# First operands of an attention loaded during the stage before it, ones written elsewhere, duplicate stores of q dropped

## The reference, cut to what matters

```python
scores = jnp.einsum('bhqd,bhkd->bhqk', qh, kh) * scale          # A
scores = scores * decay[None, None, :, :]
attn = jax.nn.softmax(scores, axis=-1)
...
scores = jnp.einsum('bhqd,bhkd->bhqk', q, k) / jnp.sqrt(jnp.float32(HD))   # B, after rope
scores = jnp.where(causal, scores, -jnp.inf)
attn = jax.nn.softmax(scores, axis=-1)
```

## Time and profile before

| | us |
|---|---|
| three runs of the kernel | 3136.64, 3138.38, 3142.13 |
| their median | 3138.38 |
| span of the profiled execution, first to last instruction | 3131.4 |

### The profile page before, as it was taken

One profiled execution on the slowest core, in us unless ns is written; L12 is line 12 of the kernel. 1 busy time (PEld: TensorE's weight loads), 2 busy tenths in 40 slices (PEclk: granted clock), 3 DMA queues, 4 the chain that ended last, 5 costly groups with the idle time before them and its releaser, 6 DMA issues. The chain is left out here.

```text
span 3131.4 us, 129400 instructions
## 1 busy us (share of the span) xinstructions
PE 2658.5 (85%) x53553; PEld 1508.1 (48%) x53553; DVE 2510.0 (80%) x7597; ACT 1876.0 (60%) x3797; POOL 1754.7 (56%) x1984
## 2 busy tenths in 40 slices
PE   5884999999999999973340899999999999999998
PEld 2441333333333333363230566666666666666665
DVE  4676899999998999766706788888888888888886
ACT  5783899999999999821000455455555555555553
POOL 5871222222222222341063788888888888888886
PEclk9895999999999999986565999999999999999999
DMA  4676344333333343094023000000000000000000
GB/s 135 235 261 178 73 106 94 93 93 99 93 90 96 94 106 94 27 276 122 0 43 89 10 12 11 8 8 11 11 11 11 11 11 11 11 11 5 11 8 11
DMA packets 179263, 209.94 MB, mean 67 GB/s; under 512 B 28592, under 2 KB 140144, under 8 KB 178416
## 3 DMA queue, kind: packets, MB, share of 16 engines
q1 hardware_dynamic: 176112, 200.25, 23.1%
q0 software_dynamic: 2560, 1.35, 0.4%
HBM read 125.10 MB, written 75.63 MB: 64 GB/s over the span
## 5 line engine op out<-in xcount | busy, mean ns | idle before, releaser
L829 ACT ACTIVATE at_pA<-at_ps 128x512 f32<-128x512 f32 x1024 | 551.9, 614 | 83.8 <-DVE at_ps L882 77.1
L891 DVE CUSTOM_DVE_ANT_0 at_junk<-at_ps,w_cmask 128x512 f32<-128x512 f32 (+3 forms) x1024 | 463.4, 485 | 104.4 <-PE at_ps L732 97.1
L882 DVE TENSOR_TENSOR at_ps<-at_ps,w_ratio 128x128 f32<-128x128 f32 (+3 forms) x1024 | 451.2, 491 | 4.7 <-PE at_ps L726 3.1
L701 POOL TENSOR_SCALAR_AFFINE_SELECT at_pB<-at_pB 128x128 f32<-128x128 f32 x256 | 75.4, 294 | 639.6 <-ACT at_pB L835 637.5
L835 ACT ACTIVATE at_pB<-at_ps 128x512 f32<-128x512 f32 (+1 forms) x768 | 379.4, 531 | 53.0 <-PE at_ps L739 47.7
L1980 POOL TENSOR_TENSOR sc_rb<-sc_rb,v_sin 128x512 f32<-128x512 f32 x256 | 326.6, 1276 | 37.6 <-DVE sc_ra L2220 36.2
L2016 PE MATMUL sc_ps<-sc_xT,v_wqkv 128*128 128x512 f32 x512 | 286.1, 641 | 3.9 <-PEq L56 1.4
L726 PE MATMUL at_ps<-at_aq,at_ak 72*128 72x512 bf16 x1024 | 278.3, 388 | 2.7 <-DMA at_ak<-parts_scratch 2.4
L2179 ACT COPY sc_skN<-sc_ps 128x512 f32<-128x512 f32 x128 | 75.1, 587 | 323.6 <-PE sc_ps L2068 323.6
L1975 POOL TENSOR_TENSOR sc_sk<-sc_ee,sc_relu 128x512 f32<-128x512 f32 x128 | 167.0, 1304 | 180.5 <-ACT sc_ee L2170 180.3
L739 PE MATMUL at_ps<-at_bq,at_bk 75*128 75x512 bf16 (+3 forms) x1024 | 265.7, 302 | 1.5 <-ACT at_pB L835 0.9
(11 more groups left out here) (316 smaller groups left out, 5937.4 us busy)
## 6 DMA issues: line engine op xcount, KB each, us to landing
parts_scratch<-fr_parts SPq DMA_DIRECT2D x64, 384.0 KB, 4.1
at_bq<-parts_scratch SPq DMA_DIRECT2D x192, 96.0 KB
at_bk<-parts_scratch SPq DMA_DIRECT2D x192, 96.0 KB
at_aq<-parts_scratch SPq DMA_DIRECT2D x192, 96.0 KB
at_ak<-parts_scratch SPq DMA_DIRECT2D x192, 96.0 KB
v_scratch<-fr_v SPq DMA_DIRECT2D x32, 352.0 KB, 4.3
at_v<-v_scratch SPq DMA_DIRECT2D x32, 352.0 KB, 3.6
parts_scratch<-fr_parts SPq DMA_DIRECT2D x32, 256.0 KB, 3.9
```

Of the source, the lines that this page charges most:

```text
L829: act.activation(pA[:, n % A_RING, j * S:(j + 1) * S], src, ACT.Exp).then_inc(exped, 1)
L882: dve.tensor_tensor(src[:, 0:wide], src[:, 0:wide], W["ratio"][:, S - wide:S], ALU.mult).then_inc(tilted, 1)
L891: ins = dve.tensor_tensor_reduce(junk[:, P * j * (j + 1) // 2:P * (j + 1) * (j + 2) // 2], src[:, col:col + wide], W["cmask"][:, S - wide: ...
```

## The change

A new function `first_operands` takes buffers for A's group 0 and for B's groups 0 and 1, and the semaphores of all groups' loads, ahead of `front`, and both stages get them as `O`. All groups now have buffers of their own in place of a slice of one tensor. In `front`, DVE writes the ones of B's groups 0 and 1 first of all, and SP at the end of step 3 issues the loads of these three pairs, 24 transfers, all of batch 0. In `attend`, POOL writes the ones of B's groups 2 to 5, one tile after another, and SP's first loads are A group 1, v of batch 0, B group 2, v of batch 1, B groups 3 to 5, each of B's behind its tile's ones. `parts_scratch` has three slots in place of five, the second store of q is gone, and the rotated copies 1 and 2 of q are loaded by two transfers each (16 and 8 rows, or 8 and 16), so a pair is eight transfers. `attend` no longer has DVE's `memset`.

```diff
+def operand(sp, c, dst, b, t, rot, g, sem_):
+    src = c["parts_d"][b * 4 + t:b * 4 + t + 1]
+    for first, count, row in (((0, 3, 0),), ((1, 2, 0), (0, 1, 2)), ((2, 1, 0), (0, 2, 1)))[rot]:
+        rows = src[:, first:first + count].rearrange("o s (d h) f -> (o s d) h f", h=H)[:, 4 * g:4 * g + 4]
+        sp.dma_start(dst[HD * row:HD * (row + count)], rows).then_inc(sem_, 16)
+def load_pair(sp, c, q, k, n, t, sem_):
+    for a in range(3):
+        rows = slice(3 * HD * a, 3 * HD * (a + 1))
+        operand(sp, c, q[rows], n // NG, t, a, n % NG, sem_)
+        operand(sp, c, k[rows], n // NG, t + 1, 0, n % NG, sem_)
...
-                    sp.dma_start(dst[:, 0:3], parts[:, b % PR, t]).then_inc(parts_out[b % PR], 16)
-                    if t % 2 == 0:
-                        sp.dma_start(dst[:, 3:5], parts[:, b % PR, t, 0:2]).then_inc(parts_out[b % PR], 16)
+                    sp.dma_start(dst, parts[:, b % PR, t]).then_inc(parts_out[b % PR], 16)
...
+                    if k == PR:
+                        sp.wait_ge(parts_out[0], 64)
+                        sp.wait_ge(early_ones, EARLY)
+                        load_pair(sp, c, O["bq"][0], O["bk"][0], 0, 2, O["b_in"][0])
+                        load_pair(sp, c, O["aq"][0], O["ak"][0], 0, 0, O["a_in"][0])
+                        load_pair(sp, c, O["bq"][1], O["bk"][1], 1, 2, O["b_in"][1])
...
+                for n in range(EARLY):
+                    dve.memset(O["bk"][n][64:ROWS + 3], 1.0).then_inc(early_ones, 1)
...
-                sp.wait_ge(ones, 1)
-                load_b(0)
-                load_a(0)
-                load_b(1)
+                load_a(1)
                 load_v(0)
-                load_a(1)
-                load_b(2)
-                load_v(1)
-                for n in range(3, B_GROUPS):
+                for n in range(EARLY, B_GROUPS):
+                    sp.wait_ge(ones, n - EARLY + 1)
                     load_b(n)
+                    if n == EARLY:
+                        load_v(1)
...
+                for n in range(EARLY, B_GROUPS):
+                    pool.memset(bk[n][64:ROWS + 3], 1.0).then_inc(ones, 1)
+                    pool.wait_ge(ones, n - EARLY + 1)
...
-                                pe.wait_ge(a_in[g % A_GROUPS], 96 * (g // A_GROUPS + 1))
+                                pe.wait_ge(a_in[g % A_GROUPS], PAIR_IN * (g // A_GROUPS + 1))
...
-                dve.memset(bk[64:ROWS + 3], 1.0).then_inc(ones, 1)
...
-    shapes = dict(xn=((NB, S, D), F32), v=((NB * 2, P, NC * VW), F32), parts=((NB * 4, 5, P, S), BF16),
+    shapes = dict(xn=((NB, S, D), F32), v=((NB * 2, P, NC * VW), F32), parts=((NB * 4, 3, P, S), BF16),
```

More of the change, by code:

```diff
@@ L127, with front @@
 LIMIT = 64.0
-def front(nc, c, W, nb):
+A_GROUPS, B_GROUPS = 2, 6
+EARLY = 2
+def operand(sp, c, dst, b, t, rot, g, sem_):
[8 more added lines that the diff above has]
+        operand(sp, c, k[rows], n // NG, t + 1, 0, n % NG, sem_)
+PAIR_IN = 16 * 8
+def front(nc, c, W, O, nb):
     with ExitStack() as ctx:
@@ L211, in _ @@
                     sp.wait_ge(v_out[n], 32 * len(range(n, nb, PR)))
-                    sp.wait_ge(parts_out[n], 96 * len(range(n, nb, PR)))
+                    sp.wait_ge(parts_out[n], 64 * len(range(n, nb, PR)))
             @block.gpsimd
@@ L514, in attend @@
         LAG = 8
-        A_GROUPS, B_GROUPS = 2, 6
-        aq, ak = sb("aq", [ROWS, A_GROUPS, 4, S], BF16), sb("ak", [ROWS, A_GROUPS, 4, S], BF16)
-        bq, bk = sb("bq", [ROWS + 3, B_GROUPS, 4, S], BF16), sb("bk", [ROWS + 3, B_GROUPS, 4, S], BF16)
+        aq, ak = (O[t] + [sb(f"{t}{n}", [ROWS, 4, S], BF16) for n in range(1, A_GROUPS)] for t in ("aq", "ak"))
+        bq, bk = (O[t] + [sb(f"{t}{n}", [ROWS + 3, 4, S], BF16) for n in range(EARLY, B_GROUPS)] for t in ("bq", "bk"))
         v = sb("v", [P, 2, 2, NC, VW])
@@ L529, in attend @@
         PV, JOB = 6, 7
-        a_in = [sem(f"a_in{n}") for n in range(A_GROUPS)]
-        b_in = [sem(f"b_in{n}") for n in range(B_GROUPS)]
+        a_in, b_in = O["a_in"], O["b_in"]
         m_in = [sem(f"m_in{n}") for n in range(B_GROUPS)]
@@ L608, in _ @@
             def _(sp):
[L609 to L613, removed]
                 def load_a(n):
@@ L617, in load_a @@
                         sp.wait_ge(filled, nth["filled", ("A2", 4 * (n - A_GROUPS) + 3)])
[L618 to L621, removed]
+                    load_pair(sp, c, aq[n % A_GROUPS], ak[n % A_GROUPS], n, 0, a_in[n % A_GROUPS])
                 def load_b(n):
@@ L625, in load_b @@
                         sp.wait_ge(filled, nth["filled", ("T2", 4 * (n - B_GROUPS) + 3)])
[L626 to L629, removed]
+                    load_pair(sp, c, bq[n % B_GROUPS], bk[n % B_GROUPS], n, 2, b_in[n % B_GROUPS])
                 def load_m(n):
@@ L725, in scores_a @@
                     slot = n // 4 % A_GROUPS
-                    pe.matmul(ps[:, BANK[f"A{j}"], :], ak[:, slot, n % 4, j * P:(j + 1) * P], aq[:, slot, n % 4], start=True, stop=True).then_inc(filled, 1)
+                    pe.matmul(ps[:, BANK[f"A{j}"], :], ak[slot][:, n % 4, j * P:(j + 1) * P], aq[slot][:, n % 4], start=True, stop=True).then_inc(filled, 1)
                 def scores_m(kind, n):
@@ L2335, in weights, with first_operands @@
     return W
+def first_operands(nc, ctx):
+    sb = lambda n, rows: ctx.enter_context(nc.sbuf_tensor("at_" + n, [rows, 4, S], BF16))
+    sem = lambda n: ctx.enter_context(nc.semaphore("at_" + n))
+    return dict(aq=[sb("aq0", ROWS)], ak=[sb("ak0", ROWS)], bq=[sb(f"bq{n}", ROWS + 3) for n in range(EARLY)],
+                bk=[sb(f"bk{n}", ROWS + 3) for n in range(EARLY)],
+                a_in=[sem(f"a_in{n}") for n in range(A_GROUPS)], b_in=[sem(f"b_in{n}") for n in range(B_GROUPS)])
 def shape_constants():
@@ L2406, in program @@
         fold_weights(nc, c, W)
-        front(nc, c, W, NB)
-        attend(nc, c, W, NB)
+        with ExitStack() as first:
+            O = first_operands(nc, first)
+            front(nc, c, W, O, NB)
+            attend(nc, c, W, O, NB)
         tail(nc, c, W, NB)
```

13 lines of the change are left out of this document (7 added, 6 removed).

## The result

The changed kernel takes 3119.04 us (median of 4 runs, 3117.76 to 3123.61) beside 3140.26 (4 runs, 3136.64 to 3143.98) for the kernel before: a ratio of 0.9932, with a 95% interval from 0.9918 to 0.9946. That is 21.2 us by the medians, against 21.7 in the forecast's sum, and 17 to 26 by the interval. The profiled execution is the one of 3123.61, with a span of 3121.8, so 1.8 us lie around the span. By the same 1.8 the profiled execution of before took about 3133, some 5 us less than the median of 3138.38 that the forecast went by. So I compare the profiles stage by stage, and the times by medians. One execution of all those reported here, the profiled one of the kernel with both repairs timed last, took 5355.08 us, with PE busy for 5068 us where that kernel's other profile has 2666; it is left out of every median and reading.

A forecast was written before the change was run, and what follows sets the result against it. PE bounds the running attention, but the front-attention seam leaves 27 us without computing except a `memset`. 22.0 - 1.5 + 1.5 - 0.3 = 21.7 us gained, 3138.4 to 3116.7 us, range 3110 to 3127; chance 0.70.

The forecast's parts named there:

- `memset`, loads and last store, to the first matmul: Front-attention seam: `memset` and loads leave the path, 15.9 us gained; last store lands at 252.0 instead of 256.1, 4.1 gained.
- A scores behind it: Attention start: head 0's A scores follow the first matmul by 1.3 us instead of 3.3, 2.0 gained.
- ones in the front: DVE at the front's start: two tiles written during the 3.63 us wait for x, 0.3 us lost, 3.4 without that cover.
- block of 24 loads: SP's queue after step 3: held 9.4 us, step 4 5.2 late, ACT 0 to 2.5 late; 1.5 us lost.
- fewer bytes, and what fronts differ by: Front: fewer store bytes shorten ACT's five waits for `parts` stores, 6.6 us in all; 1.5 gained, bounds 0 and 6.6.
- the front pays for the queue: Rival, chance 0.14: the inserted loads delay step 4 by the full 9.4 us, nothing swallowed; 3124.6 us.
- POOL's four tiles: Attention start: POOL's ones writes slow DVE by 0 us, at worst 6.9.
- the slower rival: Attention, chance 0.02: finer loads become the bound, 0.8 us more on each of 64 groups, 51 us added; 3168 us.
- the clock's low stretch: Attention's first heads: low clock moves with the work; rival, chance 0.10, rise two heads sooner, 3113.9, or later, 3121.
- The span lies 7.0 below the median: Whole program: profiled span 3131.4 against median 3138.38; the same 7.0 us taken around the new span of 3109.7.
- 0.2%, or 6.3 us: Whole program: about the smallest time difference that a measurement here can tell.

The follow-up runs named there:

- both repairs: Changed kernel with early load pairs at steps 4, 6 and 8 and the two ones `memset`s at step -3: 3107.86 us; side by side 3103.63 against 3110.43.
- the changed kernel's two other profiles: The changed kernel run again with nothing edited: 3115.96 us; and once more beside the kernel with both repairs, on another chip: 3110.43 us.
- tiny transfers: Kernel with both repairs plus 24 transfers of 1 KB in step 3, where the changed kernel has its 24 loads: 3116.46 us from two runs.
- the moved `memset`s: Changed kernel with DVE's two ones `memset`s behind its first batch instead of ahead of it: 3115.91 us, ratio 0.9937.
- the three kernels without duplicates and without the block: Changed kernel with no early loads, 3119.43 us; with the loads spread over steps 4, 6 and 8, 3115.49; with both repairs, 3107.86.
- the two with before's front: The kernel before, 3140.26 us, and the same with its one `memset` cut into six, each B load waiting for its own tile, 3128.73.
- the three comparisons: Changed kernel against the kernel before, timed three times: ratios 0.9932, 0.9932 (nothing edited) and 0.9940 (side by side with both repairs).

## Why the prediction came out

The time was right, and the path that the prediction named is the one that gave the gain. That the sum came so close is in part luck: two terms were off by several microseconds in opposite directions. At the A scores of head 0, by the first two profiles:

| term | forecast | measured |
|---|---|---|
| `memset`, loads and last store, to the first matmul | 15.9 + 4.1 = 20.0 | 27.3 - 3.9 = 23.4 |
| A scores behind it | 2.0 | 3.3 - 0.7 = 2.6 |
| ones in the front | -0.3 | -1.1 |
| block of 24 loads | -1.5 | -5.6 |
| fewer bytes, and what fronts differ by | +1.5 | -0.9 |
| sum | 21.7 | 18.4 |

In the changed kernel's two other profiles the A scores come 21.3 and 21.2 sooner than before. There the block costs 6.4 and 6.0 and the ones 1.5 and 1.3, the seam is the same, and the last row but one is +3.2 and +2.4: it is what is left over, and holds the spread of the fronts.

**The seam: right in kind, too small by 4.0.** I took the `memset`'s place in the profile, 259.80, for its start, and so counted the 3.7 us ahead of it as barrier. In the changed kernel the last store lands at 258.7 (the page's wait list has SP wait 2.4 behind its last issue, which ends at 256.33), and POOL and PE start at 259.82 and 259.86: landing to work takes 1.1. The rest of the 3.7 belonged to the `memset`, whose record is shorter than its work: 2.14 a tile makes 12.8, 2.5 more than the 10.30 recorded. A further 0.9 came from the stores: the duplicates cost 5.0 when put back, not 4.1. The Trainium skill (VectorE: DVE Perf Modes, Zero memsets can be issued as uint32) says that a memset takes a cycle per element whatever its type. The trace agrees in that the cost goes by elements: 2.14 us for a tile of 2048 is 1.04 ns each, and the 10.7 us gained by five tiles fewer ahead of the first load are 1.04 ns each again; DVE's cycle itself is shown by no run here.

**The block of loads: the step that failed.** The forecast had the next burst late by 5.2 and ACT's wait at 2.5 of it, and took 1.5, "more than half", hoping that PE's later wait would swallow some. The burst came 6.3 late, as an issue took 0.43 and not 0.39. The stores landed in 6.2 to 7.6 where I took 4.0, because I counted the loads' issue and put their time on the DMA engines at nothing: by the tiny transfers that is the larger part, an estimated 3.4 of the 5.3 that ACT waits. And nothing was swallowed: PE was made late itself, ACT's next wait for it became 3.20 where it had been 2.46, the step became 5.6 longer, and the steps behind it kept their length to within 1 us. So a sign of error that the prediction names, a wait of ACT for stores over 3 us near 118 that later batches do not win back, did appear. This was the rival "the front pays for the queue" in its size class, at 5.6 of its 9.4, but its mechanism, the held queue alone, was the smaller part.

**The ones: mis-sized, 0.3 for 1.1.** I set two recorded durations, 3.44, into a gap of 3.63. Two starts 2.14 apart need 4.3, and they begin behind the weights' folding. The experiment that moves them gives back 1.3 in ACT's first normalization; at the seam and at the scan no gain of that size is shown. POOL's four tiles cost nothing, as forecast: DVE's multiplications take 492 ns in the mean of the first 360 us, 493 before, and a single one of 512 columns takes 698 ns beside POOL's writes and 700 in the kernel before.

**Fewer bytes: not settled, of the size forecast.** From ACT's first normalization to DVE's last piece the front took 218.0, 217.5 and 216.3 in the three kernels without duplicates and without the block, and 220.0 and 218.7 in the two with before's front. That is 1 to 4, with 1.5 forecast, and fronts of one kernel differ by up to 3. ACT's waits for stores did go, from 6.6 and 10.8 in the two to 0, 0 and 1.2 in the three; but the front with 10.8 of them was the shorter of its two, so a wait there is not a loss of the same size.

**The rest.** Heads without T work still take 4.12, no matmul of the changed kernel's profile waits for the finer loads, so the slower rival has nothing to stand on, and the clock's low stretch moved along with the work, 31.5 us long from the first matmul, under the 35 that I named as a sign of error. From the A scores of head 0 to those of head 12 it takes 53.6 before and 53.2 after, so the clock neither gave nor took anything here. In single executions it does: the second low stretch lasted about 14 us and not 7 in the profiles of the moved `memset`s and of both repairs, and there, with both repairs, heads 0 to 12 took 56.8. With tiny transfers on top of the same repairs it was 7 again, so it doesn't belong to the edit. "The span lies 7.0 below the median" was no property of the program: 1.8 of it lies around the span, and about 5 was that one execution. For the same reason 0.2%, or 6.3 us, is about what medians can tell here (the ratios' intervals reach 0.13 to 0.26% to either side), and too fine for single executions.

By the marks of its three profiles the change is worth 18.5, 21.3 and 21.2 at the A scores and 17.9, 19.1 and 16.4 at the scan, and by the ratios of the three comparisons 21.4, 21.3 and 18.8, each with an interval some 9 to 13 us wide. So 16 to 21 is what the profiles show, with one profile of before. The closeness of 21.7 to 21.2 owes something to the errors' opposite signs: 4.0 too little at the seam, and in the front 0.3 lost by the forecast where 7.6, 4.7 and 4.8 were lost.

## What to carry to other kernels

Moving loads ahead of a barrier pays what they waited there, but they take a queue that others use: count the time that the block holds the issuing queue and the time that the transfers keep the DMA engines busy, find who waits for the next store behind it, and put the loads in small portions into several steps: here one block paid back half of what the early loads gained at the seam, and three portions paid back next to nothing. Before pricing a long instruction, look at the spacing of its repeated neighbours: where starts lie further apart than the recorded duration, the spacing is the price. And before moving work, try the cheap cut: splitting one wide `memset` so that the first load waited for its own sixth alone gave 9 of some 20 us.

## What the runs showed of the hardware that was not expected

DVE's `memset` of 2048 elements in 11 rows is recorded with 1.76 us, but two of them start 2.14 apart, at the front's start and in six in a row alike; the one of 12288 elements is recorded with 10.30 and held its place for 12.8 by the same spacing, starting ahead of its record: with five of the six tiles out of the way the first matmul came 10.7 us sooner behind the front.

Loads of 8 to 24 rows issued one behind another kept the DMA engines 83% busy and moved 139 GB/s (111 to 117 us of the changed kernel; 169 from 107 to 117), where stores of 128 rows moved 347 in 111 to 117 us of before; stores behind them on the same queue landed in 6.2 to 7.6 us in place of 4.0, and behind 24 transfers of 1 KB in 3.8 to 4.2. A transfer of 1 KB took SP no less time to issue than one of 32 to 96 KB: 12.46 / 24 = 0.52 against (116.22 - 105.80) / 24 = 0.43.

One and the same scan took from 1403 to 1417 us in profiled executions; what the executions differ in stays open.
